# A pre-norm transformer stack on Trainium2: ScalarE makes the attention's shifted sequences, and TensorE transposes the deviations out of a column read with stride zero

## The reference

```python
# adapter, per sequence (language_ids chooses the weights)
h = relu(x @ w1 + b1)
x = x + h @ w2 + b2
x = (x - mean(x)) * rsqrt(var(x) + 1e-5) * gamma + beta

# six layers; shift_tokens delays the second half of the features by one token
def shift_tokens(t):
    a, s = split(t, 2, -1)
    return concatenate([a, pad(s, one row of zeros in front)[:, :-1]], -1)

for i in range(6):
    x = attn_layer(shift_tokens(x), Wqkv[i], ...) + x   # 16 heads of 64, l2-normed q and k, rotary,
                                                        # softmax over windows of 32 and the one before
    x = ffn_layer(shift_tokens(x), ...) + x             # layer norm, 128 -> 2 x 341, gelu gate, -> 128
```

## Time and profile before

| | us |
|---|---|
| median of 3 runs | 5840.7 |
| lowest and highest | 5830.07 and 5843.88 |
| the profiled execution, its own time | 5848.61 |
| span of the profiled execution | 5846.8 |
| mean granted TensorE clock | 0.937 of full |
| the adapter with its norm, about | 1535 to 1597 |
| the six layers, about | 1603 to 5250, some 604 each |

### The profile page before, as it was taken

One profiled execution on the slowest core, in us unless ns is written; L12 is line 12 of the kernel. 1 busy time (PEld: TensorE's weight loads), 2 busy tenths in 40 slices (PEclk: granted clock), 3 DMA queues, 4 the chain that ended last, 5 costly groups with the idle time before them and its releaser, 6 DMA issues. The chain is left out here.

```text
span 5846.8 us, 128835 instructions
## 1 busy us (share of the span) xinstructions
PE 5079.1 (87%) x43296; PEld 3299.7 (56%) x43296; DVE 3854.6 (66%) x6824; ACT 3254.7 (56%) x9898; POOL 3175.1 (54%) x1509
## 2 busy tenths in 40 slices
PE   4995899447589999999999999999999899987864
PEld 1331677334357765776577657765777477744542
DVE  2112000554289967997799769986999599956888
ACT  0000000332178866887588858884888488844432
POOL 0000000112389957996699759984999399930018
PEclk9999999759699999999999999999999999998975
DMA  7676555011100000000000000000000000000000
GB/s 208 166 181 143 117 108 109 24 59 50 38 7 0 0 16 5 0 0 16 5 0 0 16 5 0 0 0 20 1 0 0 20 1 0 0 16 14 7 2 14
DMA packets 271956, 199.78 MB, mean 34 GB/s; under 512 B 179032, under 2 KB 254264, under 8 KB 265336
## 3 DMA queue, kind: packets, MB, share of 16 engines
q1 hardware_dynamic: 202073, 119.60, 8.9%
q10 hardware_dynamic: 67487, 71.25, 4.2%
q0 software_dynamic: 2048, 4.20, 0.2%
HBM read 131.83 MB, written 63.16 MB: 33 GB/s over the span
## 5 line engine op out<-in xcount | busy, mean ns | idle before, releaser
L1800 POOL TENSOR_TENSOR rs<-ss,minus_half 128x16 f32<-128x16 f32 x386 | 1127.7, 2921 | 170.9 <-DVE ss L1877 168.8
L1718 ACT ACTIVATE s_ps<-s_ps,low 128x128 f32<-128x128 f32 x3072 | 1064.0, 352 | 1.1 <-DVE low L1888 1.1
L1798 POOL TENSOR_TENSOR t<-t 128x1024 f32<-128x1024 f32 x386 | 911.5, 2361 | 149.4 <-DVE t L1866 149.4
L1805 POOL TENSOR_TENSOR qk<-t,rs 128x1024 f32<-128x1024 f32 x386 | 734.3, 1902 | 60.5 <-POOL rs L1800 23.7
L1718 ACT ACTIVATION_READ_ACCUMULATOR s_ps<-s_ps,low 128x1 f32 x3072 | 673.3, 219 | 0.0
L1888 DVE TENSOR_REDUCE low<-s_ps 128x4 f32<-128x512 f32 x768 | 494.4, 685 | 150.0 <-PE s_ps L1546 150.0
L1897 DVE TENSOR_TENSOR p<-s_ps,rec 128x512 f32<-128x512 f32 x768 | 530.7, 691 | 30.5
L1860 DVE TENSOR_TENSOR t<-qk_ps,rot 128x1024 f32<-128x1024 f32 x386 | 472.4, 1224 | 95.1 <-PE qk_ps L1512 89.5
L1695 ACT ACTIVATE sq<-qk_ps 128x1024 f32<-128x1024 f32 x386 | 395.3, 1024 | 249.1 <-DVE t L1866 249.1
L1732 ACT ACTIVATE pT<-pT_ps 128x512 f32<-128x512 f32 x768 | 457.2, 595 | 104.2 <-PE pT_ps L1552 68.5
L264 PE MATMUL h_ps<-h_x,h_w 9*128 9x512 bf16 x4096 | 441.5, 628 | 84.3 <-DMA h_w<-rows_w1s 63.6
(11 more groups left out here) (404 smaller groups left out, 8781.6 us busy)
## 6 DMA issues: line engine op xcount, KB each, us to landing
h_x<-rows_xs SPq DMA_DIRECT2D x512, 72.0 KB
rows_hs<-h_parts ACTq DMA_DIRECT2D x88, 384.0 KB, 7.1
z_fm<-rows_hs SPq DMA_DIRECT2D x128, 144.0 KB
x_fm<-rows_hs SPq DMA_DIRECT2D x128, 144.0 KB
wqkv<-in_wqkv SPq DMA_DIRECT2D x7, 1536.0 KB, 6.6
o_w<-rows_exs ACTq DMA_DIRECT2D x512, 18.0 KB
rows_xs<-z_fm ACTq DMA_DIRECT2D x12, 384.0 KB, 5.5
rows_exs<-s_exp ACTq DMA_DIRECT2D x9, 512.0 KB, 6.7
```

The lines of the kernel that those rows point to most:

```text
L1718: ins = act.activation(s_ps[:, e, i * P:(i + 1) * P], s_ps[:, e, i * P:(i + 1) * P], ACT.Exp, bias=low[:, c % 2, e, i:i + 1], scale=-1.0, ...
L1798: pool.tensor_tensor(t1[:, i, :], t1[:, i, :], t2[:, i, :], ALU.add).then_inc(s_["t12"], 1)
L1800: pool.tensor_tensor(rs[:, i, :], ss[:, i, :], R.minus_half[:, 0:2 * UH], ALU.pow).then_inc(s_["rs"], 1)
L1805: pool.tensor_tensor(qk[:, i, :].rearrange("p (h d) -> p h d", d=DH), t1[:, i, :].rearrange("p (h d) -> p h d", d=DH), rs[:, i, :].unsquee ...
```

## The change

ScalarE gets the shift of each next sequence, as two Copy activations, between keep_v and keep_o. Their lag is 0, and all other ACT stages get a lag larger by two, so they run two units behind it and ACT's written-out end has six slots in place of four; what followed the slots (`after`) moves with them. ACT waits at the top of a layer for the last feed-forward residual of the layer before. Unit 0's shift stays on DVE (`first_shift`). POOL no longer makes `diag`; PE turns each of the four columns of rstd, read as a 128x128 matrix with stride zero, by a transpose into the same PSUM tile. The tile diag and its semaphore are gone: rstd now waits for the spread of the group before.

```diff
@@ level2_cond (spread and rstd_; the same in level2_layers, lines 1607 to 1616 and 1810 to 1818)
                 def spread(k):
-                    pe.wait_ge(s_["diag"], at(k))
+                    pe.wait_ge(s_["rstd"], at(k))
                     pe.wait_ge(s_["xn"], at(k - 1))
-                    pe.matmul(r_ps[:, :], R.ones[:, :], diag[:, :, :].rearrange("p b s -> p (b s)"),
-                              start=True, stop=True).then_inc(s_["spread"], 1)
+                    for b in range(GB):
+                        mm = pe.transpose(r_ps[:, col(b)], rstd[:, b:b + 1].to_broadcast([P, P]), R.ident[:, :])
+                    mm.then_inc(s_["spread"], 1)
...
                 def rstd_(k):
                     pool.wait_ge(s_["var_eps"], at(k))
-                    pool.wait_ge(s_["diag"], at(k - 1))
+                    pool.wait_ge(s_["spread"], at(k - 1))
                     pool.tensor_tensor(rstd[:, :], var[:, :], R.minus_half[:, 0:GB], ALU.pow).then_inc(s_["rstd"], 1)
-                    pool.wait_ge(s_["rstd"], at(k))
-                    pool.wait_ge(s_["spread"], at(k - 1))
-                    pool.tensor_tensor(diag[:, :, :], R.ident[:, :].unsqueeze(1).to_broadcast([P, GB, P]),
-                                       rstd[:, :].unsqueeze(2).to_broadcast([P, GB, P]), ALU.mult
-                                       ).then_inc(s_["diag"], 1)
@@ level2_layers, ScalarE
+                def shift(k, j, c):
+                    if c % UPB:
+                        return
+                    i = (c // UPB) % 2
+                    act.wait_ge(s_["vp"], at(k - 3))
+                    act.activation(xs[0:64, i, :], R.z_fm[0:64, bass.ds(j * (P // UPB), P)], ACT.Copy)
+                    act.activation(xs[64:P, i, 1:P], R.z_fm[64:P, bass.ds(j * (P // UPB), P - 1)], ACT.Copy
+                                   ).then_inc(s_["xs"], 1)
...
                 with act.Fori(0, DEPTH) as l:
-                    pipeline(act, NU, 8, [(keep_q, 2), (keep_p1, 4), (exps1, 3), (keep_k, 2), (keep_v, 0), (keep_o, 4),
-                                          (squares, 0), (keep_p0, 3), (exps0, 2)], k0=l * NU, last=lambda i: after(l, i),
-                             early=(squares,))
+                    act.wait_ge(s_["f_res"], at(l * NG - 1))
+                    pipeline(act, NU, 8, [(keep_q, 4), (keep_p1, 6), (exps1, 5), (keep_k, 4), (keep_v, 2), (shift, 0),
+                                          (keep_o, 6), (squares, 2), (keep_p0, 5), (exps0, 4)], k0=l * NU, last=lambda i: after(l, i - 2),
+                             early=(squares, shift))
@@ level2_layers, VectorE
-                def shift(k, j, c):
-                    if c % UPB:
-                        return
-                    i = (c // UPB) % 2
-                    a, b = R.z_fm[0:64, bass.ds(j * (P // UPB), P)], R.z_fm[64:P, bass.ds(j * (P // UPB), P - 1)]
-                    dve.wait_ge(s_["vp"], at(k - 3))
-                    dve.scalar_tensor_tensor(xs[0:64, i, :], a, 1.0, a, ALU.mult, ALU.max)
-                    dve.scalar_tensor_tensor(xs[64:P, i, 1:P], b, 1.0, b, ALU.mult, ALU.max).then_inc(s_["xs"], 1)
+                def first_shift(l):
+                    a, b = R.z_fm[0:64, 0:P], R.z_fm[64:P, 0:P - 1]
+                    dve.wait_ge(s_["vp"], at(l * NU - 3))
+                    dve.scalar_tensor_tensor(xs[0:64, 0, :], a, 1.0, a, ALU.mult, ALU.max)
+                    dve.scalar_tensor_tensor(xs[64:P, 0, 1:P], b, 1.0, b, ALU.mult, ALU.max).then_inc(s_["xs"], 1)
...
-                    pipeline(dve, NU, 8, [(normalise0, 4), (shift, 0), (rotate, 1), (normalise1, 4), (rotate_swapped, 1), (lows, 3),
+                    pipeline(dve, NU, 8, [(normalise0, 4), (rotate, 1), (normalise1, 4), (rotate_swapped, 1), (lows, 3),
                                           (sums, 1), (residual, 5)], k0=l * NU,
                              first=lambda i: before(l, i), last=lambda i: after(l, i),
-                             early=(shift, rotate, rotate_swapped, sums))
+                             early=(rotate, rotate_swapped, sums))
```

More of the change, by code:

```diff
@@ L1261, in level2_cond @@
         rstd = m.sb("ad_rstd", [P, GB])
-        diag = m.sb("ad_diag", [P, GB, P])
         xn = m.sb("ad_xn", [P, GT])
@@ L1269, in level2_cond @@
         w_ps = [m.ps(f"ad_w_ps{i}", [P, 1024], BF16) for i in range(2)]
-        names = ("hid", "relu", "adapt", "sum", "center", "sq", "var", "var_eps", "rstd", "diag",
+        names = ("hid", "relu", "adapt", "sum", "center", "sq", "var", "var_eps", "rstd",
                  "spread", "xn", "z", "wT", "wTc")
@@ L1458, in level2_layers @@
         rstd = m.sb("ff_rstd", [P, GB])
-        diag = m.sb("ff_diag", [P, GB, P])
         xn = m.sb("ff_xn", [P, GT])
@@ L1473, in level2_layers @@
                  "pTc0", "pTc1", "o", "oTc", "proj", "res",
-                 "f_xs", "f_center", "f_xc", "f_sq", "f_var", "f_vare", "f_rstd", "f_diag", "f_spread", "f_xn",
+                 "f_xs", "f_center", "f_xc", "f_sq", "f_var", "f_vare", "f_rstd", "f_spread", "f_xn",
                  "f_xa", "f_z", "f_gel", "f_h", "f_down", "f_res")
@@ L1608, in spread @@
                     k = l * NG + j
-                    pe.wait_ge(s_["f_diag"], at(k))
+                    pe.wait_ge(s_["f_rstd"], at(k))
                     pe.wait_ge(s_["f_xn"], at(k - 1))
@@ L1614, in spread @@
                         pe.wait_ge(s_["p1"], at(l * NU + NU - 1))
-                    pe.matmul(r_ps[j], R.ones[:, :], diag[:, :, :].rearrange("p b s -> p (b s)"),
-                              start=True, stop=True).then_inc(s_["f_spread"], 1)
+                    for b in range(GB):
+                        mm = pe.transpose(r_ps[j][:, b * P:(b + 1) * P], rstd[:, b:b + 1].to_broadcast([P, P]),
+                                          R.ident[:, :])
+                    mm.then_inc(s_["f_spread"], 1)
                 def feed(l, j, t):
@@ L1811, in rstd_ @@
                     pool.wait_ge(s_["f_vare"], at(k))
-                    pool.wait_ge(s_["f_diag"], at(k - 1))
+                    pool.wait_ge(s_["f_spread"], at(k - 1))
                     pool.tensor_tensor(rstd[:, :], var[:, :], R.minus_half[:, 0:GB], ALU.pow).then_inc(s_["f_rstd"], 1)
[L1814 to L1818, removed]
                 norms(0, 0, 0)
@@ L1993, in tables @@
                     dve.wait_ge(s_["f_res"], at((l - 1) * NG))
-                    shift(l * NU, 0, 0)
+                    first_shift(l)
                 def turn(l, u):
```

## The result

The changed kernel takes 5768.9 us in the median of 4 runs (5753.39 to 5772.04), the kernel before 5838.0 us in its 4. The ratio is 0.9877, with a 95% interval of 0.9855 to 0.9899: 1.2% faster, 69 us. Run again later, beside other kernels, it took 5762.5 us in 5 runs (0.9878 of before, 0.9854 to 0.9902). Forecast were 5768, in a range of 5752 to 5803.

The account below looks back on a forecast made before the run. It took PE, or a loop running through it, to bound all stages; 47 us for the shift, 20.6 for the feed-forward spread and 5 in the adapter make 72.6, so 5840.7 becomes 5768 us, range 5752 to 5803.

Parts of the forecast that it names:

- The shift off DVE: Attention: removing the shift from DVE lets PE set rotation starts, ordinary pairs gaining 0.16 us; 47 us with layer starts.
- Starts of layers: Start of five layers: PE's 0.64 us wait for DVE's shift disappears, 3.2 us in all.
- ACT's copies, price zero: Attention on ACT: two copies, taken as 0.4 us, cost nothing while under 0.79 us, hidden by existing waits.
- limit of 0.79 us: ACT's cover behind keep_v, 0.37 + 0.42 us, before squares is late; each further 0.1 us costs 18.6 us.
- the two cases in which ACT decides: Attention: ACT eats the gain, 5815 us, chance 0.06; or ACT becomes the bound, up to 5872 us, chance 0.04.
- The spread: Feed-forward: four transposes replace PE's wide matmuls, 0.43 us less for each of 48 groups, 20.6 us.
- The rival of dear transposes: Feed-forward and adapter: stride-zero loads make four transposes cost 0.86 us, 5793 us, at the upper bound 5834; chance 0.07.
- The adapter: Adapter: eight spreads get shorter and the last no longer waits for POOL's diag, 5 us in all.
- The clock rival: Adapter: PE's clock stays low because transposes may not count as busy, 5781 us, chance 0.12.
- the listed sign: Adapter: a clock of 0.50 past 1569, listed among what the profile would show if the prediction was wrong.
- The signs: Profile after, whole kernel: listed marks of right (turn_q every 7.61 us, groups 9.91 apart) and wrong (squares without a wait).

Follow-up runs that it names:

- experiment 4: Changed kernel with the shift back on DVE, cut into two halves in separate places, ACT's order as before the change: 5777.6 us, 0.9899 of before.
- experiment 2: Changed kernel with ACT's two copies cut to one column of 64 partitions, same wait and signal: 5777.4 us, 0.9896 of before.

## Why the prediction was right, point by point

- **The shift off DVE, 47 us.** Measured 47.2 us by the run of the shift alone, and by stages 44.0 us in the attention where 6 x 7.3 = 44 was the sum. The mechanism held: the rotation waits for PE again, and an ordinary pair went from 15.38 to 15.22 us as forecast. That the sum fits to the microsecond is luck. A pair with a turn takes 7.78 + 7.66 = 15.44 against 15.37 and so gave 0.50 in place of 0.58, some 3 us less for 36 of them; the three intervals ahead of the loop gave 5.2 us over six layers where 6 x 0.3 was counted, some 3 us more.
- **Starts of layers, 3.2 us.** 4.8 measured. PE's waits for the shift in the layers two to six, 0.45 to 0.72 us each and 2.9 in all, are gone as forecast. What made that shift long is the collision with POOL's product that experiment 4 shows; the prediction had taken the 1.49 us as it stood. I didn't take the other 1.9 us apart.
- **ACT's copies, price zero.** Right in effect, and the size was off: 0.65 us for the two against my 0.4. I had let them overlap as the 512-column copies out of PSUM do; their starts are 0.33 us apart and each takes 0.32 and 0.30, so they don't overlap at all. The cover held them, but 0.27 us more a pair is all that was left. The prediction's limit of 0.79 us was near the 0.92 of my estimate, and its price beyond the limit would be 0.51 us a pair for copies of 1.30 us, where 0.38 was measured. The prediction's chance of 0.10 for the two cases in which ACT decides looks small against that: by an estimate from 0.92, two copies of 0.5 us instead of 0.3 would have cost some 0.1 us a pair, and the same copies two places further on in ACT's order made the kernel slower than before.
- **The spread, 20.6 us.** Groups 9.92 apart, 25.9 us for the spread alone (19 to 41 by its interval), 22.8 by stages in the whole change, of which the spacing of the residuals accounts for 20.3. Stride zero costs nothing that the rows show: four transposes hold PE for 0.44 us, as four others do. The rival of dear transposes falls.
- **The adapter, 5 us.** Its terms are in the rows: at the upper clock a spread holds PE for 0.46 us (1552.35 to 1552.81) where before it held it for 0.95 (1581.89 to 1582.84), and DVE's last product comes 2.32 us after the one before it in place of 3.57, 1.25 less against the 1.3 of the sum. Its whole is neither confirmed nor refuted, since its clock moves it by more from run to run.
- **The clock rival, 5781.** Open. Both profiles of the changed kernel have the clock at 1.00 beside transposes, in the adapter and in the feed-forward part, so transposes don't hold it down by necessity. But the run without the copies, with the same adapter code, had the listed sign nearly whole: 0.50 for the 20 us up to 1570, 0.67 in the next 20, an adapter 22.7 us longer, and a median of 5777.4 us, not far from the rival's time. The old code's two adapters, 94.0 and 94.1 us, lie between. With wide matmuls between them, these rows can't test a rule about transposes alone.
- **The signs.** DVE's 0.34 before each rotation outside the turns, 7.61 without alternation, groups 9.91, the copies at 0.3 and POOL without the product came as listed. ACT's wait before the squares was to get shorter and not go; it went, which was also listed among the signs of being wrong, and experiment 2 shows that this sign had been drawn too tight: it marked the end of one cover, with the exponentials' behind it still open.
- **The sum against the median.** 5768 against 5768.9 and 5762.5. The agreement to a microsecond is luck: single runs of the changed kernel lie between 5745 and 5777, and errors of some 3 us in the attention's terms cancel.

## What to carry to other kernels

Work on an engine that waits in each round costs only what exceeds its wait (0.56 us cost 0.16 in an ordinary pair here, and 0.24 a pair with the turns in the mean); price its removal by that excess. Before giving the work to another engine, follow all of that engine's readers in a round, not only the next one, for the place in its order decides: 0.65 us cost nothing ahead of a wait and 0.54 us behind it. Look also at what runs on POOL beside a DVE copy: the same half of a shift took 0.29 or 0.72 us by its place. Where spans of two profiles differ by more than the medians do, compare them stage by stage before crediting the change.

## What was not expected of the hardware

- Two ACT copies from SBUF to SBUF of 64x128 and 64x127 take 0.32 and 0.30 us and start 0.33 us apart, without overlap, while copies of 128x512 out of PSUM start 0.48 apart though each takes 0.63. One of 64x1 takes 0.21, so most of the 0.32 doesn't depend on the columns.
- A DVE operation of 64x127 with both inputs in SBUF took 0.29 us by itself and 0.48 to 1.88 when it started within POOL's 128x1024 product, always ending 0.15 us after it. Within POOL's power of 128x16, 2.91 us long and reading SBUF too, the one of 64x128 took its plain 0.27.
- The clock in one and the same stretch of code, with PE busy all the time, was 0.97 in one run and 0.50 in another.
